# A gated attention block with expert-choice FFN: the last group's experts in reverse order, a ring of w1 quarters, w2's split parts side by side, and copies of the routing moved to ScalarE

## What is computed

```python
x = x + tanh(g_xattn) * xattn(layernorm(x), ctx)     # per token: 16 heads x 16 heads
x = x + tanh(g_ffn)   * ffn(layernorm(x))

def ffn(x):                                          # 8 experts, D 256, hidden 1024
    probs = softmax(x @ gate_w.T)
    g, m = top_k(probs over the tokens, k = 64)      # each expert picks 64 tokens of each batch
    h = gelu(x[m] @ w1[e])                           # exact gelu
    out.at[m].add(g * (h @ w2[e]))
```

## Time and profile before

| | |
|---|---|
| median of three runs | 699.21 us (699.01 to 699.41) |
| profiled execution | 700.73 us, span of its instructions 698.7 us |
| TensorE (PE) busy | 660.8 us, 95% |
| VectorE (DVE) | 597.7 us, 86% |
| GpSimd (POOL) | 535.4 us, 77% |
| ScalarE (ACT) | 433.0 us, 62% |
| mean granted clock of TensorE | 0.976 |
| DMA | 160.96 MB, 230 GB/s over the span |

### The profile page before, as it was taken

The page is one execution under the profiler, slowest core; times in us unless marked ns, Lnnn a source line. Parts: engine busy times, 40 slices in busy tenths (PEclk is TensorE's granted clock), DMA queues, the critical chain, the costliest instruction groups (busy, mean ns, idle before and its releaser), DMA issues.

```text
span 698.7 us, 11584 instructions
## 1 busy us (share of the span) xinstructions
PE 660.8 (95%) x3921; PEld 539.8 (77%) x3921; DVE 597.7 (86%) x786; ACT 433.0 (62%) x1081; POOL 535.4 (77%) x498
## 2 busy tenths in 40 slices
PE   8999989978799999989999999989999999999996
PEld 5566566534688888878888888868888899999995
DVE  6999999899999999998999999999999251586763
ACT  5677677655777777766777778747766533232321
POOL 4899899897878888988888889888898516435343
PEclk8999999989999999999999999989999999999999
DMA  3876798461558787776788877767777858999993
GB/s 126 304 260 207 229 306 261 177 242 49 190 181 247 241 268 237 221 229 187 222 245 250 242 242 226 234 173 240 227 233 223 269 177 281 327 311 303 322 269 38
DMA packets 97073, 160.96 MB, mean 230 GB/s; under 512 B 8171, under 2 KB 74486, under 8 KB 97014
## 3 DMA queue, kind: packets, MB, share of 16 engines
q1 hardware_dynamic: 84006, 142.78, 61.1%
q0 software_dynamic: 12288, 16.79, 12.9%
q10 hardware_dynamic: 720, 0.66, 0.3%
HBM read 126.63 MB, written 33.55 MB: 229 GB/s over the span
## 4 chain that ended last, share of the span: by engine, by line
PE 67%; DMA 10%; issue 7%; POOL 6%; DVE 6%; ACT 3%; POOLq 0%; DVEq 0%; ACTq 0%
PE bank L1176 21%; PE bank L1159 19%; DMA out_dram<-ys,ids 8%; PE bank L1086 6%; PE bank L1203 4%; PE bank L1106 4%; PE bank L1039 3%; PE bank L1193 3%; DVE prod_v L492 2%; POOL prod_p L344 2%; PE bank L1145 2%; DVE co L494 1%; PE bank L1118 1%; DMA xg<-xn_scratch,ids 1%; POOL tree_a L352 1%
## 5 line engine op out<-in xcount | busy, mean ns | idle before, releaser
L1159 PE MATMUL bank<-xin,w1in 128*128 128x256 f32 x1536 | 205.0, 291 | 5.3 <-issue 4.9
L1159 PEld LDWEIGHTS bank<-xin,w1in 128*128 128x128 f32 x1536 | 193.8, 196 | 6.8 <-issue 6.1
L1176 PE MATMUL bank<-w2s,hT 128*128 128x256 f32 x768 | 175.4, 382 | 0.0
L415 POOL DMA_INDIRECT out_dram<-ys,ids x64 | 105.0, 1640 | 76.8 <-ACT ys L865 57.7
L1176 PEld LDWEIGHTS bank<-w2s,hT 128*128 128x128 f32 x768 | 142.4, 190 | 17.7
L851 ACT ACTIVATE hT<-bank 128x512 f32<-128x512 f32 x128 | 76.0, 597 | 107.7 <-PE bank L1159 107.1
L494 DVE TENSOR_REDUCE co<-prod_v 128x208 f32<-128x3328 f32 (+2 forms) x32 | 109.7, 3428 | 1.1
L492 DVE TENSOR_TENSOR prod_v<-bank,Ex 128x3328 f32<-128x3328 f32 (+2 forms) x32 | 109.6, 3424 | 0.1
L352 POOL TENSOR_TENSOR tree_a<-prod_p 128x512 f32<-128x512 f32 (+2 forms) x64 | 85.8, 1341 | 4.7
L401 POOL DMA_INDIRECT xg<-xn_scratch,ids x64 | 63.9, 998 | 31.8 <-issue 17.0
L344 POOL TENSOR_TENSOR prod_p<-kvs,q 128x1024 f32<-128x1024 f32 (+2 forms) x28 | 80.1, 2859 | 8.1 <-ACT q L819 6.4
(11 more groups left out here) (157 smaller groups left out, 1150.4 us busy)
## 6 DMA issues: line engine op xcount, KB each, us to landing
w1in<-w_parts SPq DMA_DIRECT2D x128, 512.0 KB, 5.3
w2s<-in_L_ffn_w_dram SPq DMA_DIRECT2D x32, 1024.0 KB, 5.7
w_parts<-w1s SPq DMA_DIRECT2D x32, 512.0 KB, 3.3
w1raw<-in_L_ffn_w_dram SPq DMA_DIRECT2D x32, 256.0 KB, 4.4
out_dram<-x SPq DMA_DIRECT2D x32, 128.0 KB, 4.2
xn_scratch<-xn SPq DMA_DIRECT2D x32, 128.0 KB, 2.5
xt<-in_x_dram SPq DMA_DIRECT2D x31, 128.0 KB, 5.2
ct<-in_ctx_dram SPq DMA_DIRECT2D x28, 128.0 KB, 4.7
```

The lines of the kernel that those rows point to most:

```text
L415: pool.indirect_dma_start(out=out_rows[:, :], out_offset=bass.IndirectOffsetOnAxis(ap=ids[:, g % 2, p * E + e:p * E + e + 1], axis=0), in_ ...
L1159: ins = pe.matmul(HB[k % 2][:, D * f:D * (f + 1)], w1in[:, k, w, c, P * f:P * (f + 1)].bitcast(f32r), xin[:, n % 2, x_, c, :], start=(m == ...
L1176: ins = pe.matmul(dst, hT[:, n % 2, f, cols], w2s[:, n % 2, f, :], start=(f == 0), stop=(f == FC - 1))
```

## The change

- The last group's experts run in reverse order, 7 to 0. Expert step 24 is then expert 7 again, as step 23, and uses the w1 and the split w2 that are already there.
- From step 25 on, w1's quarters go to a ring of seven places: three new ones (over GpSimd's product buffer, free after the last tile) and the four of before.
- Expert steps 22 and 23 also run in split form; TensorE's order around them is changed.
- w2's parts lie side by side, and hh multiplies both in one matmul of 512 columns; its bank holds two half sums, which ScalarE and VectorE (`add_halves`) put together in `ys`. hl by w2's high part stays at 256 columns. The y banks alternate between expert steps. The very last call of `outputs` keeps three matmuls of 256.
- `hh` is written by ScalarE, by a second gelu from PSUM, in place of VectorE's cast.
- Routing: the copy of the probabilities and the gates' scaling move from VectorE to ScalarE. In the routing steps x comes into S0 by the identity matmul, and VectorE takes 13 heads of values in place of 12.
- GpSimd's `add_rows` runs four expert steps behind `gather` in the drain, before three.

```diff
-    START, EARLY, LATE, FIRST_ROUTING, ROUTING = (11, 11), (12, 11), (12, 13), (4, 12), (4, 12)
+    START, EARLY, LATE, FIRST_ROUTING, ROUTING = (11, 11), (12, 11), (12, 13), (4, 13), (4, 13)
+    n2 = NE - E
+    RING = Q + 3
+    expert = lambda n: n % E if n < n2 else NE - 1 - n
-    with_x = lambda t: t < N0 - 2
+    with_x = lambda t: t < N0 - 2 or routing(t + 1)
...
+            def load_w1_ring(n, k):
+                i = turn(n, k)
+                if i < RING - Q:
+                    sp.wait_ge(cop_done, NT)
+                else:
+                    sp.wait_ge(h_psum, Q * (n2 + 1) + i - RING + 1)
+                sp.dma_start(w1_quarter(i), w1x_d[Q * expert(n) + k]).then_inc(ring_loaded[i % RING], 16)
...
             load_w2(n1)
-            for n in range(n1 + 1, NE):
+            load_w2(n1 + 1)
+            for k in range(Q):
+                load_w1(n1 + 1, k)
+            for k in range(RING - Q):
+                load_w1_ring(n2 + 1, k)
+            load_w2(n2 + 1)
+            for n in range(n2, NE):
                 for k in range(Q):
-                    load_w1(n, k)
-                load_w2(n)
+                    i = Q * (n - n2) + k + RING - Q
+                    if i < Q * (E - 1):
+                        load_w1_ring(n2 + 1 + i // Q, i % Q)
+                if n > n2 and n + 1 < NE:
+                    load_w2(n + 1)
...
+            def add_halves(n):
+                g, e = n // E, expert(n)
+                for p in range(PR):
+                    if (n, p) == (NE - 1, 1):
+                        return
+                    dve.wait_ge(y_half, 2 * (n - n1) + p + 1)
+                    col = gts[:, g % 2, p * E + e:p * E + e + 1]
+                    dve.scalar_tensor_tensor(ys[:, n % 2, p, :], y_bank(n, p)[:, D:2 * D], col, ys[:, n % 2, p, :],
+                                             op0=ALU.mult, op1=ALU.add).then_inc(y_ready, 1)
...
             def gelu(n, k):
                 act.wait_ge(h_psum, Q * n + k + 1)
+                if n >= n1:
+                    act.activation(hh[n % 2][:, 2 * k:2 * k + 2, :].rearrange("p f n -> p (f n)"), HB[k % 2][:, :], ACT.Gelu).then_inc(hh_ready, 1)
...
                     if p == 0 and f % (FC // Q) == 0:
                         pe.wait_ge(hl_ready, Q * m + f // (FC // Q) + 1)
-                    pe.matmul(dst, hh[n % 2][:, f, cols], w2h[n % 2][:, f, :], start=(f == 0), stop=False)
-                    pe.matmul(dst, hh[n % 2][:, f, cols], w2l[:, n % 2, f, :], start=False, stop=False)
-                    ins = pe.matmul(dst, hl[:, n % 2, f, cols], w2h[n % 2][:, f, :], start=False, stop=(f == FC - 1))
+                    if whole:
+                        pe.matmul(y[:, :], hh[n % 2][:, f, cols], w2_parts[v][:, :, f, :], start=(f == 0), stop=False)
+                    else:
+                        pe.matmul(y[:, 0:D], hh[n % 2][:, f, cols], w2hi[v][:, f, :], start=(f == 0), stop=False)
+                        pe.matmul(y[:, 0:D], hh[n % 2][:, f, cols], w2lo[v][:, f, :], start=False, stop=False)
+                    ins = pe.matmul(y[:, 0:D], hl[:, n % 2, f, cols], w2hi[v][:, f, :], start=False, stop=(f == FC - 1))
...
             route_columns(gl)
             hidden(n + 2, 0)
             hidden(n + 2, 1)
-            outputs(n + 1, 0)
-            outputs(n + 1, 1)
-            token_transposes(n + 3)
             hidden(n + 2, 2)
             hidden(n + 2, 3)
+            outputs(n + 1, 0)
+            token_transposes(n + 3)
+            outputs(n + 1, 1)
```

More of the change, by code:

```diff
@@ L43, in flamingo_gated_block_kernel @@
     gl = G - 1
[L44 removed]
+    n2 = NE - E
+    RING = Q + 3
+    expert = lambda n: n % E if n < n2 else NE - 1 - n
+    turn = lambda n, k: Q * (n - n2 - 1) + k
+    w2_slot = lambda n: n % 2 if n < n2 else (n + 1) % 2
+    split_turn = lambda n: n - n1 if n < n2 else n - n1 - 1
     summed = lambda t: 0 < t < N0 - 1
@@ L49, in flamingo_gated_block_kernel @@
     order = {u: j for j, u in enumerate(plain)}
-    with_x = lambda t: t < N0 - 2
-    x2_steps = lambda t: 3 * t - min(t, N0 - 2)
+    routing = lambda s: s % TG == 2 and s > TG
+    with_x = lambda t: t < N0 - 2 or routing(t + 1)
+    x2_steps = lambda t: 3 * t - sum(with_x(u) for u in range(t))
     heads = lambda t: (START if t == 0 else FIRST_ROUTING if t == N0 - 1 else EARLY if t < N0 - 1 else
@@ L471, in _ @@
             add_rows(n1 - 1)
-            add_rows(n1)
             for n in range(n1 + 4, NE):
                 gather(n)
-                add_rows(n - 3)
-            for n in range(NE - 3, NE):
+                add_rows(n - 4)
+            for n in range(NE - 4, NE):
                 add_rows(n)
@@ new lines, in split_experts @@
+            def split_experts():
+                split_w2(n1, (0,))
+                low_hidden(n1, 0)
+                low_hidden(n1, 1)
+                split_w2(n1, (1,))
+                low_hidden(n1, 2)
+                low_hidden(n1, 3)
+                split_w2(n1 + 1, (0,))
+                low_tokens(n2)
+                split_w2(n1 + 1, (1,))
+                low_hidden(n1 + 1, 0)
+                low_hidden(n1 + 1, 1)
+                low_hidden(n1 + 1, 2)
+                low_hidden(n1 + 1, 3)
+                low_tokens(n2 + 1)
+                add_halves(n1)
+                for n in range(n2, NE):
+                    low_hidden(n, 0)
+                    low_hidden(n, 1)
+                    if n2 < n and n + 1 < NE:
+                        low_tokens(n + 1)
+                    if n > n2:
+                        split_w2(n)
+                    low_hidden(n, 2)
+                    low_hidden(n, 3)
+                    add_halves(n - 1)
+                add_halves(NE - 1)
@@ L1171, in outputs @@
                         pe.wait_ge(y_ready, 2 * n)
-                cols = slice(P * p, P * (p + 1))
-                dst = XT[:, 0:D] if (n, p) == (NE - 1, 1) else YB[:, D * p:D * (p + 1)]
+                if n < n1:
+                    for f in range(FC):
+                        ins = pe.matmul(YB[:, D * p:D * (p + 1)], hT[:, n % 2, f, cols], w2s[:, n % 2, f, :], start=(f == 0), stop=(f == FC - 1))
+                    ins.then_inc(y_psum, 1)
+                    return
+                m, v = n - n1, w2_slot(n)
@@ L1174, in outputs @@
+                y, whole = y_bank(n, p), (n, p) != (NE - 1, 1)
                 for f in range(FC):
-                    if not last:
-                        ins = pe.matmul(dst, hT[:, n % 2, f, cols], w2s[:, n % 2, f, :], start=(f == 0), stop=(f == FC - 1))
-                        continue
                     if p == 0 and f % (FC // 2) == 0:
-                        pe.wait_ge(w2l_ready, 2 * m + f // (FC // 2) + 1)
+                        pe.wait_ge(w2l_ready, 2 * split_turn(n) + f // (FC // 2) + 1)
```

135 lines of the change are left out of this document (81 added, 54 removed).

## The result

The changed kernel takes 698.44 us (median of 20 runs, 693.84 to 700.75); the kernel before took 699.49 us in the 20 runs beside it. The medians differ by 1.05 us. The ratio is 0.9971 (95%: 0.9960 to 0.9983), which is 2.0 us (1.2 to 2.8), and the means differ by 1.8; these part because the single runs spread unevenly over 7 us, before over 3. So the change gives between 1 and 2 us where 5.8 were forecast.

A forecast was written before the change was run, and what follows sets the result against it. TensorE was taken as the bound: its own instructions in the drain, idling behind VectorE's choice of tokens in routing steps. -2.3 - 3.9 + 0 + 0.15 + 0.2 = -5.8 us gave median 693.4 us, range 690.9 to 697.6.

The forecast's parts named there:

- Part 1: Drain, outputs of experts 22 and 23: split form saves 1.1 to 1.15 us of TensorE per expert, -2.3 us.
- nearly late: Drain, gather of expert 24: rows needed at 585.5 us land at 584 to 586; counted 0.
- Part 2: Drain, w2's parts merged into 512-column matmuls: 27 ns saved per block, 144 times, -3.9 us.
- Rival (a): Drain merging: the 13 ns does not hide behind a wide matmul, part gives 0 to 2 us; 696.3 us, chance 0.30.
- Part 3: Drain, no w1 and w2 load for expert 24 and a ring of seven: cover only, 0 us.
- Part 4: The end: the 0.9 us pause goes, but the chain of scatters sets the finish, 12.8 us after outputs(30,1); +0.15 us.
- Part 5: Routing steps: -0.65 us in step 10, +0.4 each in steps 18 and 26; together +0.15 to +0.2 us.
- (c): Drain: split does not fit where VectorE is late or DMA engines bound; 1 or 2 us given back, 695; chance 0.07.
- (d): Drain: TensorE stands for expert 24's rows or w1's quarters and low clock follows; slower, 701.9 us, chance 0.08.
- a gain or loss of 1.5 us: Routing steps: TensorE's 1.87 us idle and the low clock behind it counted unchanged, with this much either way possible.

The follow-up runs named there:

- e3: The changed kernel with w2's two parts multiplied by separate matmuls of 256 columns into one half bank, without VectorE's addition of halves; 698.80 us, ratio 0.9979.
- e10: The changed kernel with its whole routing part undone and the route matmuls issued ahead of hidden(n, 2); 695.95 us, ratio 0.9936 to the kernel before.
- e6: The changed kernel with the route matmuls issued ahead of hidden(n, 2) in the routing steps, identity matmul kept; 694.60 us, ratio 0.9923 to the kernel before.
- e8: The changed kernel without the routing steps' identity matmuls and with a ring of five w1 quarters in place of seven; 697.38 us, ratio 0.9964.
- e4: The changed kernel without the identity matmuls in the routing steps, 13 heads and ScalarE's copies kept; 696.39 us, ratio 0.9956 to the kernel before.
- e2: The kernel before with the change's routing part alone (13 heads, residual by identity matmul, copies on ScalarE), drain as before; 701.38 us, ratio 1.0028.
- e1: The changed kernel with its whole routing part undone (12 heads, residual, probabilities' copy and gates on VectorE), drain still changed; 697.48 us, ratio 0.9969.
- e7: The changed kernel without the routing steps' identity matmul and with the route matmuls ahead of hidden(n, 2); 694.59 us, ratio 0.9934 to the kernel before.

## Why the prediction was wrong

**Part 1 (experts 22 and 23 in split form, -2.3): right.** The step of 13.08 us is 11.65. The stretch before it, which has the other expert, went from 20.73 to 19.59. Together that is 2.57 us; in e3, without merging, it is 2.33 (19.70 and 11.78). (In e3 0.5 us of this is lost again in the stretch between, 6.65 for 6.18, where it waits for rows.) The cover held in the profiled run, but "nearly late" was right too, as e10, e3 and e6 show.

**Part 2 (merging, -3.9): the step that failed first.** "Then a block takes 0.213 + 0.12 = 0.333": the matmul of 512 columns took 0.233, and the block 0.353. Of the surcharge of 13 ns I saw on 256 columns (0.12 against 0.107) about half goes with the columns: 512 less 256 columns is 0.233 - 0.12 = 0.113 us, 0.44 ns a column against 0.417 at 2.4 GHz, which is 6 ns on 256. The part that a merge saves is the other 7 ns, not 27, so 144 x 7 ns = 1.0 us in place of 3.9, and e3 has 6 ns. I took the middle of a range on rows of float32, where the one float32r row, with its 0.237 us, said otherwise. Rival (a), 0 to 2 us, came true. The Trainium skill's page "TensorE: Matmul & The Clock Gate" (section "Back-to-back issue gap") gives a lone warm matmul a fixed cost of 2.5 ns; this stream has about 7, and 0.233 us for 512 columns where the page's formula gives 0.216. It was the nearer estimate all the same, by 0.4 against 3.9 us where 1.0 was measured.

**Part 3 (ring, weights used twice, 0): right within what was measured**; by the traces of e8 and e4 the ring is worth at most 0.4 us. Not foreseen is the 0.08 us per expert of other places.

**Part 4 (the end, +0.15): right.** 12.8 us from outputs(30,1) to the end, and the scatter chain is what is late.

**Part 5 (routing steps, +0.15 to +0.2): wrong, +1.4 by e2.** The mechanism was named: the ids wait of the earlier trace rows grew from 0.37 to 1.41 us in step 26, as forecast ("about 1.5"). The price was wrong. I let the identity cost its own 0.43 us (it takes 0.54) and booked VectorE's savings against it. But once TensorE's order sets `ids`, these savings count nothing in steps 18 and 26, and the gather becomes last instead of VectorE. The low clock is not what was added: the 24 matmuls behind the stand take 4.59 and 5.46 us before in these steps, 4.43 and 4.60 after. In step 10, where all of the 0.65 us was to count, the lists come no sooner, `ids` 0.32 (14.67 to 14.35 after con(9)) and the next `con` 0.15 (23.59 to 23.44). Nor did I read how far TensorE already lags in steps 17 and 25 (4.2 to 4.9 us). By the medians the identity alone costs 2.5 us (after against e4); the two copies on ScalarE and the head give 1.1 us (e4 against e1), 1.7 with the early order (e7 against e10), each known to a microsecond or two. And in step 18, "the same order" as step 26, the rows I left out had no wait for `ids` at all: there the change made one.

**Rivals.** (a) is what happened in part 2. (c) did not: no w2 split was late for TensorE. (d) did not in the measured sense; its stands are there, up to 1.06 us for rows and 0.64 for w1, under the 2 us from which I let it decide. None of them had the routing steps as a loss, though the text had left "a gain or loss of 1.5 us" open there, and the range did not hold it.

**The sum put right:** -2.3 - 1.0 - 0.6 (places, 0.08 for seven experts) + 0.15 and about half a microsecond back for late rows is -3.2 for the drain, and +1.4 makes -1.8; the medians have -1.05, the ratio 1.2 to 2.8 us less. Each part has its own error of up to a microsecond.

**The better kernel** is e6 or e7, 694.6 us: the change with the route matmuls moved ahead of one quarter of the hidden layer. That is 5.5 us under before, three to five times what the change itself gave.

## What to carry to other kernels

When work is taken off the engine that looks last, follow the chain from the other side as well: in a routing step the gather hangs on a matmul of 0.6 us whose place in TensorE's order decides whether the savings count. Moving it ahead of one quarter was worth 4.5 us in the changed kernel. And follow a saving up to the thing that is waited for: in two of the three routing steps the rounds began 0.3 us earlier and the lists came no earlier. Where an engine lags behind its partner by a steady few microseconds, read that lag step by step before pricing anything put on it. For a surcharge that could be per column or per instruction, go by the one row that has the format in question, however awkward it is to read, and not by tidy rows of another format.

## What was not expected of the hardware

- A float32r matmul of 512 columns takes 0.233 us where one of 256 takes 0.12, so widening saves 6 to 7 ns.
- The pace goes with the buffer the operand lies in: 24 matmuls of 256 columns take 2.80 us (0.1167 each) on w1 in the new places and 2.88 (0.12) in the old ones. Why was not tried.
- Two traces of the same main loop (after and e3) differ by 1.5 us in TensorE's lag in step 11, and still by 0.75 in step 17.
- Expert 24's rows, the first of them asked for some 6.5 to 8 us ahead of their use, were in time in some traces, 0.24 us late in one (e3) and 1.06 in another (e10).
- A VectorE instruction of 0.18 us took 0.8 beside an addition on GpSimd and ended with it, in both kernels.
